# A graph network's first pass on one core: some VectorE operands kept in a PSUM bank, source counts summed per block

## What is computed

```python
x = _layernorm(x + _L0_gnn_ref(x, edge_weight, edge_weight_n2, ..., src, dst), axis=-1)
x = _layernorm(x + _L1_gnn_ref(x, edge_index, edge_attr_32, ...), axis=-1)
x = _layernorm(x + _L2_gnn_ref(x, edge_index, ...), axis=-1)
x = _layernorm(x + _L3_gnn_ref(x, edge_index, edge_attr_32, ...), axis=-1)
```

```python
def _spmm(w, src, dst, h, n):
    return jax.ops.segment_sum(w[:, None] * h[src], dst, num_segments=n)
h_low = jax.nn.relu(_spmm(w_low, src, dst, x @ W_low, n))
h_high = jax.nn.relu(_spmm(w_high, src, dst, x @ W_high, n))
...
seg_sum = jax.ops.segment_sum(edge_attr, row, num_segments=N)
seg_max = jax.ops.segment_max(edge_attr, row, num_segments=N)
cnt = jax.ops.segment_sum(jnp.ones((edge_attr.shape[0], 1), edge_attr.dtype), row, num_segments=N)
```

## Time and profile before

| | us |
|---|---|
| median of 3 runs | 8453.33 (8445.2 to 8454.42) |
| profiled execution | 8436.37 |
| its span | 8434.7 |
| first scatter to the start of the last one | 88.0 to 2624.3 |
| POOL busy over the span | 5204.4 (62%) |
| DVE busy over the span | 5190.6 (62%) |
| PE busy over the span | 5474.9 (65%) |

### The profile page before, as it was taken

One profiled execution on the slowest core, in us unless ns is written; L12 is line 12 of the kernel. 1 busy time (PEld: TensorE's weight loads), 2 busy tenths in 40 slices (PEclk: granted clock), 3 DMA queues, 4 the chain that ended last, 5 costly groups with the idle time before them and its releaser, 6 DMA issues. The chain is left out here.

```text
span 8434.7 us, 150442 instructions
## 1 busy us (share of the span) xinstructions
PE 5474.9 (65%) x55385; PEld 4795.1 (57%) x55386; DVE 5190.6 (62%) x8479; ACT 1717.0 (20%) x2817; POOL 5204.4 (62%) x4394
## 2 busy tenths in 40 slices
PE   3555555555553434426565279999858888888887
PEld 2444444444442333425554169999847777777776
DVE  5767677667774444445555566666656666666664
ACT  0111111111111101121114110000023433434343
POOL 4888888888884787416665245555316666666660
PEclk8777777777776666657777589999958999999996
DMA  3222222222221333210003011111011111111110
GB/s 120 93 92 102 101 92 92 95 105 96 92 92 43 101 109 108 66 57 25 26 25 120 15 23 27 27 28 27 18 48 49 49 47 51 47 52 46 52 45 11
DMA packets 315448, 529.45 MB, mean 63 GB/s; under 512 B 154649, under 2 KB 246640, under 8 KB 305008
## 3 DMA queue, kind: packets, MB, share of 16 engines
q1 hardware_dynamic: 166202, 394.33, 13.5%
q0 software_dynamic: 141056, 124.52, 6.3%
q10 hardware_dynamic: 7698, 3.40, 0.2%
HBM read 447.82 MB, written 215.61 MB: 79 GB/s over the span
## 5 line engine op out<-in xcount | busy, mean ns | idle before, releaser
L319 POOL DMA_INDIRECT pay_d<-row,place x1632 | 2040.2, 1250 | 582.2 <-issue 577.7
L2020 POOL DMA_INDIRECT m_from_src<-from_src_d,m_row x510 | 639.9, 1255 | 779.4 <-PE m_win L2067 399.7
L399 PE MATMUL win<-onehot,val 128*128 128x128 f32 x4998 | 803.9, 324 | 374.9 <-DVEq L497 369.6
L399 PEld LDWEIGHTS win<-onehot,val 128*128 128x128 f32 x4998 | 728.2, 231 | 515.7 <-DVEq L497 401.8
L1630 POOL DMA_INDIRECT g_x<-xg_d,g_row x510 | 645.9, 1266 | 587.0 <-PE g_win L1650 355.5
L1650 PE MATMUL g_win<-g_hot,y_part 128*128 128x128 bf16 x14994 | 850.1, 220 | 138.3 <-DVE g_hot L1675 100.1
L1650 PEld LDWEIGHTS g_win<-g_hot,y_part 128*128 128x128 bf16 x14994 | 844.4, 98 | 143.8 <-DVE g_hot L1675 101.0
L644 POOL DMA_INDIRECT r_x<-in_x,r_row x510 | 614.2, 1204 | 254.2 <-issue 156.0
L2023 POOL DMA_INDIRECT m_from_dst<-from_dst_d,m_row x510 | 620.5, 1217 | 155.6 <-issue 155.6
L1061 POOL DMA_INDIRECT sorted_d<-s_row,s_place x510 | 510.0, 1000 | 310.3 <-DVE s_place L1155 165.5
L370 PE MATMUL pair<-hot_hi,hot_lo 128*128 128x392 bf16 (+3 forms) x1632 | 263.8, 334 | 636.3 <-DVE hot_hi L435 636.3
(11 more groups left out here) (396 smaller groups left out, 11230.0 us busy)
## 6 DMA issues: line engine op xcount, KB each, us to landing
scan_d<-in_none SPq DMA_DIRECT2D x51, 1034.2 KB
lo_row<-lo_d SPq DMA_DIRECT2D x51, 1024.0 KB
m_grid<-pay_d SPq DMA_DIRECT2D x52, 882.0 KB, 5.0
pay_d<-in_fill SPq DMA_DIRECT2D x51, 882.0 KB
grid<-pay_d SPq DMA_DIRECT2D x51, 882.0 KB, 4.7
pay_d<-in_fill SPq DMA_DIRECT2D x51, 720.0 KB
row<-in_pay SPq DMA_DIRECT2D x51, 576.0 KB
pay_d<-row,place POOLq DMA_INDIRECT x1632
```

The lines of the kernel that those rows point to most:

```text
L319: pool.indirect_dma_start(a["pay_d"][:, :], bass.IndirectOffsetOnAxis(ap=place[j][:, c:c + 1], axis=0), row[j][:, c, :], None).then_inc(ro ...
L399: mm(win[:, :], val[u % 2][:, s, :], onehot[u % 2][:, s, :], start=(u == 0 and s == 0), stop=(u == NS - 1 and s == SUB - 1))
L2020: pool.indirect_dma_start(ps_x[j][:, c, :], None, a["from_src_d"][:, :], bass.IndirectOffsetOnAxis(ap=row[j][:, c, AT_SRC:AT_SRC + 1].bitc ...
```

## The change

It concerns `placing` alone.

- The PSUM bank of `cnt` becomes `near`: columns 0 to 127 hold the column numbers, copied once at the start, the next 49 hold `pen`, and 98 more the two weights of each slot of the open grid (`weight`).
- `hots` and `messages` read the column numbers from there, L493 and L495 the weights, L503 the penalty. Each grid costs one more copy, of the weights, in `open_grid`.
- The counts per source go into the bank of `tot`, as one sum per block; the copy of `tot` to SBUF takes 49 columns more, and DVE adds them to `k.cnt_sec` in `places`. The products with zeros that began and ended the long sum fall away.

```diff
-        tot = ps("tot", [P, 512])[:, 0:2 * CB]
-        cnt = ps("cnt", [P, 512])[:, 0:NT]
-        zero = sb("zero", [P, P], bf16)
+        tot = ps("tot", [P, 512])[:, 0:2 * CB + NT]
+        near = ps("near_dve", [P, 512])
+        iota, pen, weight = near[:, 0:P], near[:, P:P + NT], near[:, 2 * P:2 * P + 2 * NT].rearrange("p (s q) -> p s q", q=2)
...
-                        for c in range(HC):
-                            mm(cnt[:, :], hot_lo[:, h * HC + c, :], hot_hi[:, h * HC + c, :], start=False, stop=False)
+                        for c in range(h * HC, (h + 1) * HC):
+                            mm(tot[:, 2 * CB:], hot_lo[:, c, :], hot_hi[:, c, :], start=(c == 0), stop=(c == CB - 1))
...
-                v.memset(zero[:, :], 0.0).then_inc(zero_set, 1)
-                v.memset(ones16[:, :], 1.0).then_inc(zero_set, 1)
+                v.memset(ones16[:, :], 1.0).then_inc(ones16_set, 1)
+                v.memset(k.cnt_sec[:, :], 0.0)
+                v.tensor_copy(iota, k.iota[:, :])
+                dve.drain()
...
-                    v.tensor_tensor(hot_lo[:, :, :], k.iota[:, :].unsqueeze(1).to_broadcast([P, CB, P]),
+                    v.tensor_tensor(hot_lo[:, :, :], iota.unsqueeze(1).to_broadcast([P, CB, P]),
...
-                    v.tensor_tensor(hot_hi[:, :, :], k.iota[:, 0:NT].unsqueeze(1).to_broadcast([P, CB, NT]),
+                    v.tensor_tensor(hot_hi[:, :, :], iota[:, 0:NT].unsqueeze(1).to_broadcast([P, CB, NT]),
...
                     v.tensor_tensor_scan(incl[:, :], k.ones[:, 0:CB], sums[:, CB:2 * CB], 0.0, ALU.mult, ALU.add)
                     dve.drain()
+                    v.tensor_tensor(k.cnt_sec[:, :], k.cnt_sec[:, :], sums[:, 2 * CB:], ALU.add)
...
                     v.tensor_scalar(held[:, :], dst_f[:, :], float(z.n), None, ALU.is_lt)
-                    dve.drain()
-                    v.tensor_scalar(pen[:, :], held[:, :], -1.0, BIG, ALU.add, ALU.mult)
+                    v.tensor_copy(weight, grid[j][:, :, AT_LOW:AT_HIGH + 1])
+                    dve.drain()
+                    v.tensor_scalar(pen, held[:, :], -1.0, BIG, ALU.add, ALU.mult)
...
-                    v.tensor_tensor(onehot[u % 2][:, :, :], k.iota[:, :].unsqueeze(1).to_broadcast([P, SUB, W]),
+                    v.tensor_tensor(onehot[u % 2][:, :, :], iota.unsqueeze(1).to_broadcast([P, SUB, W]),
...
-                    v.tensor_tensor(val[u % 2][:, :, 0:D], x, grid[j][:, s, AT_LOW:AT_LOW + 1].to_broadcast([P, SUB, D]),
+                    v.tensor_tensor(val[u % 2][:, :, 0:D], x, weight[:, s, 0:1].to_broadcast([P, SUB, D]),
...
-                                    grid[j][:, s, AT_HIGH:AT_HIGH + 1].to_broadcast([P, SUB, D]), ALU.mult)
+                                    weight[:, s, 1:2].to_broadcast([P, SUB, D]), ALU.mult)
...
-                    v.tensor_tensor(tmp[:, :, :], grid[j][:, :, 0:F], pen[:, :].unsqueeze(2).to_broadcast([P, NT, F]), ALU.add)
+                    v.tensor_tensor(tmp[:, :, :], grid[j][:, :, 0:F], pen.unsqueeze(2).to_broadcast([P, NT, F]), ALU.add)
```

More of the change, by code:

```diff
@@ L238, in placing @@
         sec = sb("sec", [P, CB])
-        sums = sb("sums", [P, 2 * CB])
+        sums = sb("sums", [P, 2 * CB + NT])
         incl = sb("incl", [P, CB])
@@ L246, in placing @@
         held = sb("held", [P, NT])
-        pen = sb("pen", [P, NT])
         tmp = sb("tmp", [P, NT, F])
@@ L267, in placing @@
         (hot_ready, lo_hot_ready, cum_ready, upto_ready, found_ready, found_read, sec_ready, tot_ready, place_ready,
-         val_ready, hot16_ready, sub_done, grid_used, drel_ready, deg_ready, zero_set, cnt_done, starts) = (
+         val_ready, hot16_ready, sub_done, grid_used, drel_ready, deg_ready, ones16_set, starts) = (
             sem(n) for n in ("hot_ready", "lo_hot_ready", "cum_ready", "upto_ready", "found_ready", "found_read",
                              "sec_ready", "tot_ready", "place_ready", "val_ready", "hot16_ready", "sub_done", "grid_used",
-                             "drel_ready", "deg_ready", "zero_set", "cnt_done", "placing_starts"))
+                             "drel_ready", "deg_ready", "ones16_set", "placing_starts"))
         NS = NT // SUB
@@ L359, in _ @@
                 mm = nc.tensor.matmul
-                pe.wait_ge(zero_set, 2)
-                mm(cnt[:, :], zero[:, :], zero[:, 0:NT], start=True, stop=False)
+                pe.wait_ge(ones16_set, 1)
                 def counts(b):
@@ L418, in _ @@
                         spread(b, u)
-                mm(cnt[:, :], zero[:, :], zero[:, 0:NT], start=False, stop=True).then_inc(cnt_done, 1)
             @block.vector
@@ L529, in _ @@
                     close_grid(b, NBK // 3 - 1, j)
-                dve.wait_ge(cnt_done, 1)
-                v.tensor_copy(k.cnt_sec[:, :], cnt[:, :])
                 v.tensor_scalar(k.n_sec[:, NBK - 1:NBK], k.n_sec[:, NBK - 1:NBK], float(z.e - z.EP), None, ALU.add)
```

## The result

The changed kernel takes 8120.0 us (median of 4 runs, 8117.1 to 8123.1) against 8449.3 us for the kernel before (4 runs, 8440.0 to 8454.4). The ratio is 0.9612, with an interval of 0.9595 to 0.9628: 329 us less, where 307 were forecast.

What follows compares the result with a forecast made beforehand. POOL's scatters, 49.8 us per block, bound the first pass; afterwards DVE at 44.05 (43.8 + 0.25) would lead POOL's 43.4, ending the pass at 2318 instead of 2625.3. Saving 307 us gives 8146 us, range 8105 to 8225.

Steps and rivals of the forecast that it cites:

- What stays on POOL, 43.4 us per block: POOL's scatters in the first pass: 40.8 unhindered, 2.1 lost beside sum and maximum, 0.5 beside L439; ends 42.0 and 45.3.
- Operation times: The 24 DVE operations per block that lose their second SBUF operand were forecast to keep their durations.
- rivals 1 and 4: PSUM operands slow DVE: 65 ns per instruction (8220 us, chance 0.11), or repeated elements at half rate (9170 us, 0.03).
- rival 2: Port still held where only the second operand is in PSUM (`val`, `tmp`): POOL 46.4 us per block, 8280 us, chance 0.06.
- rival 3: Scatters stretch for another cause than the second SBUF read, so nothing is released: 8453 us, chance 0.03.
- New work: Added on DVE per block: weights' copy 0.26 us, covered by the PE wait; sum into `cnt_sec` 0.22; larger `tot` copy 0.05.
- DVE, not POOL, is the slower one afterwards: After the change DVE needs 44.05 us per block in the first pass, against POOL's 43.4.
- the term of 1.9 us per block: DVE's gap of 5.68 us ahead of every third stage, where the loop goes round, counted in its pace.
- Rival 5: The 5.68 us gap shrinks or hides, so POOL leads at 43.4 us per block: 8127 us, chance 0.09.
- DVE's own 41.9 us per stage: DVE's time for one stage without a wait for the grid, 3.30 us of it waiting for PE.
- rival 4: DVE reads a repeated PSUM element slower than SBUF; at half rate 715 us lost, 9170 us, chance 0.03.

Runs made afterwards that it cites:

- the one-word experiment: The changed kernel with the tile of column numbers, penalty and weights in SBUF instead of PSUM: 8445.0 us, ratio 1.0003.
- the filler experiment: The changed kernel with five sums (0.97 us each) added on DVE at the start of every third stage of the loop: 8159.0 us, ratio 0.9657.

## Why the prediction was right or wrong

- **POOL sets the pace before the change, and a scatter beside two SBUF operands waits**: right, and shown by the one-word experiment.
- **What stays on POOL, 43.4 us per block**: 43.3. What is lost to DVE is 32 x (1.048 - 0.967) = 2.6 us, as summed (2.1 + 0.5). Added up over the timeline, the sum and the maximum cost 2.0 of it and L438 0.6.
- **Operation times**: no change (4425, 1090, 610 and 615 ns; 4426, 1092, 619 and 618 for the same instructions with the tile in SBUF). One PSUM element read many times over costs nothing extra, so rivals 1 and 4 fall. The Trainium skill's fixed costs ("VectorE: DVE Perf Modes", "The TRN2 errata"), 62 cycles more for a PSUM source, do not show in these durations.
- **Partial release, rival 2, and none, rival 3**: false, by the rows beside `val` and by the one-word experiment.
- **New work**: 276 ns for the weights, 225 for the sum, 53 more for the copy of `tot`; forecast 260, 220 and 50. It does not show in the time, since DVE is not the slowest.
- **"DVE, not POOL, is the slower one afterwards"**: wrong. The step that failed is the term of 1.9 us per block for the gap where the loop goes round. I took a gap of the kernel before as a property of the loop, and an edit ahead of the loop removes it; in the changed kernel it is 0.6 us per round, 0.2 per block. DVE left alone then needs about 42.9 us per block by the filler experiment, and POOL's 43.3 decide. Rival 5 named this case with 0.09 and 8127 us, and it came so.
- **DVE's own 41.9 us per stage**: too low. It came from a single stage. The kernel before has 15 stages without a wait for the grid between 330 and 2480 us; they take 41.9 to 43.5 us, 42.5 in the mean, with 3.3 to 5.1 us of waiting for PE, 4.0 in the mean. The stage of the earlier trace rows is among the shortest. The filler experiment says the same: 8159 us with only 5.0 of the 5.68 us put back, where the prediction had 8146 with all of it.
- The predicted 8146 is 26 us above the measured 8120, in the range. That it comes so close is in part luck. The two terms for DVE err in opposite directions, and the sum put DVE only 0.65 us per block above POOL, so that naming the wrong engine cost little.
- A slip that changes nothing: rival 4 decides from a rate lower by more than a fifth, not a quarter, since 5.7 us more on 20.6 is 1.28 times the duration.

## What to carry to other kernels

Where GpSimd issues indirect transfers back to back and sets the pace, look in the timeline at what VectorE does beside the long ones. Where it has operations with two tensor inputs in SBUF, move the small one of the two to PSUM; here one copy at the start and one per block were enough. Move all neighbours at once, since a transfer freed in one place runs into the next. Take an engine's own pace from all stages in which it does not wait, not from one. And a gap at a loop's end is not a cost to sum with until a kernel with a few instructions more ahead of the loop shows it too.

## What the runs showed that was not expected

A bf16 comparison of one tensor with a number (L438, 1.28 us) holds a scatter as well, though it has only one tensor operand. How long depends on where the scatter starts. Of the 50 that L438 stretches in the changed kernel, 35 start 0.17 us or more after it does; they end 0.83 to 0.85 us after its end, like those beside two SBUF operands (998.87, 1.65 us). The other 15 start within 0.06 us of its start and end 0.12 to 0.13 us after its end (955.95, 1.38 us). Why these come off earlier is open.

And by the estimate from the filler experiment the pass has only 0.4 us between its two slowest engines: a saving on POOL of more than that per block would have to come with one on DVE.
